# A fused two-layer attention, mixture and feed-forward kernel: late expert weights in halves, rows two tiles ahead, projections two heads earlier

## The reference, cut to what matters

```python
x = x + L0_xattn(layernorm(x), ctx, ctx, mask, ...)   # 16 heads of 16, over the 256 positions of a sequence
x = x + L0_ffn(layernorm(x), router_w, ...)           # 16 experts, top 4 of each token, hidden 256
x = x + L1_xattn(layernorm(x), ctx, ctx, ...)         # 16 heads of 16, over the 16 sequences at one position
x = x + L1_ffn(layernorm(x), w_gate, w_up, w_down)    # silu gate, hidden 768
```

## Time and profile before

| | us |
|---|---|
| median of three runs | 1487.99 |
| the profiled execution | 1475.79 |
| its span, first to last instruction | 1473.9 |

### The profile page before, as it was taken

How to read it: one execution, slowest core, us unless ns; L and a number is a source line. 1 busy time by engine, 2 the same in 40 slices (tenths; PEclk the granted TensorE clock), 3 DMA queues, 4 the chain that set the end, 5 groups by cost and what they waited for, 6 DMA issues and landing times. The chain is left out here.

```text
span 1473.9 us, 34906 instructions
## 1 busy us (share of the span) xinstructions
PE 1153.6 (78%) x11011; PEld 871.1 (59%) x11012; DVE 972.4 (66%) x2207; ACT 741.7 (50%) x1455; POOL 825.2 (56%) x983
## 2 busy tenths in 40 slices
PE   3788999999860478899999996137887888849997
PEld 2456666666540366789998885125666666625554
DVE  4878878888630477566668894446777887426652
ACT  2367667676650255455555553114555666624442
POOL 5213366766576566577767772677667772005442
PEclk9889999999985699899999999577999999979999
DMA  6533442321110146543333342654475542122221
GB/s 181 123 94 99 123 91 73 91 80 51 43 41 8 49 143 155 84 124 114 114 114 110 100 115 72 144 137 123 131 202 141 140 131 64 42 72 72 86 71 58
DMA packets 138997, 147.59 MB, mean 100 GB/s; under 512 B 39848, under 2 KB 114648, under 8 KB 138840
## 3 DMA queue, kind: packets, MB, share of 16 engines
q1 hardware_dynamic: 112144, 95.45, 22.9%
q0 software_dynamic: 17920, 37.84, 11.1%
q10 hardware_dynamic: 8800, 12.59, 3.1%
HBM read 81.82 MB, written 38.40 MB: 82 GB/s over the span
## 5 line engine op out<-in xcount | busy, mean ns | idle before, releaser
L465 ACT ACTIVATE l_pt<-l_ps_t 128x512 f32<-128x512 f32 (+1 forms) x512 | 242.8, 492 | 222.0 <-PE l_ps_t L882 214.3
L735 DVE TENSOR_REDUCE l_mx<-l_ps_s 128x2 f32<-128x512 f32 (+1 forms) x512 | 275.6, 549 | 106.5 <-PE l_ps_s L917 103.2
L1371 PE MATMUL cp_ps_g<-cp_xt,ro_wexp 128*128 128x256 f16 x1920 | 228.9, 277 | 27.0 <-ACT cp_xt L1311 17.1
L1371 PEld LDWEIGHTS cp_ps_g<-cp_xt,ro_wexp 128*128 x1920 | 185.6, 99 | 56.2 <-issue 32.8
L1229 POOL DMA_INDIRECT cp_rows<-moe_rows,cp_now x160 | 163.9, 1025 | 93.9 <-POOL cp_now L1224 66.1
L384 POOL DMA_INDIRECT l_picked<-expert_rows,l_slots x128 | 142.0, 1110 | 38.6 <-issue 37.2
L408 POOL DMA_INDIRECT row_tokens<-l_token_id,ro_pos x128 | 125.8, 983 | 42.4 <-issue 42.3
L1287 DVE TENSOR_SCALAR cp_gate<-cp_ps_g,ex_g_bias 128x256 f32<-128x256 f32 x160 | 69.9, 478 | 89.7 <-PE cp_ps_g L1371 89.7
L917 PE MATMUL l_ps_s<-ro_wexp 96*128 96x256 f16 x512 | 103.3, 287 | 25.1 <-issue 8.1
L1320 ACT CAST cp_a_hi<-cp_act_f 128x512 f16<-128x512 f32 x80 | 49.4, 618 | 142.1 <-DVE cp_act_f L1296 140.5
L1234 POOL TENSOR_TENSOR cp_a_lo<-cp_act_f,cp_a_hi 128x512 f16<-128x512 f32 x80 | 95.8, 1197 | 35.8 <-ACT cp_a_hi L1320 34.6
(11 more groups left out here) (246 smaller groups left out, 2835.5 us busy)
## 6 DMA issues: line engine op xcount, KB each, us to landing
expert_rows<-cp_yout SPq DMA_DIRECT2D x80, 256.0 KB
l_cin<-in_ctxT SPq DMA_DIRECT2D x32, 256.0 KB
x<-l_yout SPq DMA_DIRECT2D x64, 128.0 KB
ro_wexp<-l_nat SPq DMA_DIRECT2D x48, 128.0 KB
ro_wexp<-l_nat SPq DMA_DIRECT2D x96, 64.0 KB
l_qs<-l_nat SPq DMA_DIRECT2D x48, 128.0 KB
l_ks<-l_nat SPq DMA_DIRECT2D x96, 64.0 KB
ro_raw<-in_gate_up ACTq DMA_DIRECT2D x10, 512.0 KB, 4.7
```

The costliest lines, as they stand in the source:

```text
L465: nc.scalar.activation(pt[:, h % 8], ps_t[:, at % 2, :, 0:span], ACT.Exp).then_inc(exp_done, 1)
L735: nc.vector.reduce_max(mx[:, n % 2, :, 8 * (k % 2) + k // 2], ps_s[:, at % 2, :, 0:span], AX_X).then_inc(max_done, 1)
L1371: last = nc.tensor.matmul(ps_g[:, b, m], route.wexp[:, bass.ds(e, 1), cols:cols + P].rearrange("p o n -> p (o n)"), xt[:, b, part, c], sta ...
```

## The change

1. Layer 0: experts 0 to 7 are split one at the end of each of the iterations u = 1 to 8, and experts 8 and 9 are loaded in u = 10 (before: u = 3).
2. Both attentions: the transposes of x move from k = 0 to k = 15 of the iteration before; high and low of x from k = 1 to k = 0, q products to k = 2, 3, their high and low to k = 4. The k products start at K_AT (7 in layer 0, 6 in layer 1; before 8), their high and low at K_AT + 2, v products at K_AT + 4, the copy to `v1` at K_AT + 6.
3. Layer 0, GpSimd: the eight scatters stand together at the end of the iteration, and for unit u-3 (before: four and four, for u-4).
4. Layer 1: VectorE makes `invert` and `weigh` of k = 5 ahead of that head's `add_expert`. GpSimd sets its constants in u = -4 (before: -5), and there the gather comes ahead of `first_norm`.
5. Expert tiles: late experts are split in halves, one half (gate and up, or down) a step, from step -2 to step 13; the low half stands behind tile i's work on VectorE. ScalarE's order in step i is sigmoid of i, high half, copy of tile i+2's rows, a_hi of i, output of i-2. The down weights get their own load semaphore.

```diff
-        EXPERTS_AT = {-3: (0,), -2: (1, 2), -1: (3, 4), 0: (5, 6), 1: (7,)} if routing else {}
+        EXPERTS_AT = {u: (u - 1,) for u in range(1, EARLY + 1)} if routing else {}
...
+        K_AT = 7 if routing else 6
...
-                    if routing and live(u - 4):
-                        scatter(u - 4, 0)
-                    if u > -5:
-                        if u > -4:
-                            gather(u + 5)
+                    if routing:
                         first_norm(u + 4)
                         if u == -4:
-                            gather(u + 5)
-                            if routing:
-                                constants()
+                            constants()
                     else:
                         gather(u + 5)
-                        if not routing:
+                        if u == -4:
                             constants()
+                        first_norm(u + 4)
...
-                    if routing and live(u - 4):
-                        scatter(u - 4, 1)
+                    if routing and live(u - 3):
+                        for q in range(QT):
+                            scatter(u - 3, q)
...
-                        n = u + 3
-                        if k == 0 and live(n):
+                        n = u + 4
+                        if k == 15 and live(n):
                             pe.wait_ge(xn_done, c1 + 2 * n + 2)
                             pe.wait_ge(v1_done, c1 + n)
...
-                        if k in (8, 9) and live(n):
+                        if k in (K_AT, K_AT + 1) and live(n):
                             pe.wait_ge(clo_done, c1 + n + 1)
                             pe.wait_ge(ql_done, c1 + n + 1)
...
-                return EARLY + i // 2 if isinstance(i, int) and i % 2 == 0 and 0 <= i // 2 < LATE else None
+                return EARLY + (i + 2) // 2 if isinstance(i, int) and 0 <= (i + 2) // 2 < LATE else None
...
+                        e = late_expert(i)
+                        if e is not None:
+                            dve.wait_ge(e_high, i + 3)
+                            part = 1 + 2 * (i % 2)
+                            nc.vector.scalar_tensor_tensor(route.part(e, part), route.raw_parts(e)[i % 2], WS, route.part(e, part - 1), ALU.mult, ALU.subtract).then_inc(e_low, 1)
...
                     def step(i, b4):
                         b = b4 % 2
-                        if live(i, 1):
-                            act.wait_ge(xt_done, at(i + 1))
-
-                            act.wait_ge(gu_done, at(i - 1))
-                            nc.scalar.copy(xt[:, 1 - b], ps_x[:, 1 - b]).then_inc(xt_copied, 1)
+                        if isinstance(i, int) and i == -2:
+                            copy_rows(0, 0)
                         if live(i, 0):
                             act.wait_ge(gate_done, at(i, 2))
 
                             act.wait_ge(act_done, at(i - 2))
                             nc.scalar.activation(sg[:, b], gate[:, b], ACT.Sigmoid, scale=ALPHA / WS).then_inc(sg_done, 1)
+                        split_half(i)
+                        if live(i, 2) and (not isinstance(i, int) or i > -2):
+                            copy_rows(i + 2, b)
+                        if live(i, 0):
                             act.wait_ge(act_done, at(i))
```

More of the change, by code:

```diff
@@ L519, in step @@
                             norm_high(u - 2)
-                        if k == 1 and live(u + 3):
+                        if k == 0 and live(u + 3):
                             act.wait_ge(xt_done, c1 + u + 4)
@@ L547, in step @@
                         n = u + 3
-                        if k == 14 and live(n):
+                        if k == K_AT + 6 and live(n):
                             act.wait_ge(v_done, c1 + n + 1)
@@ L559, in step @@
                         if k == 8:
-                            for e in EXPERTS_AT.get(u, ()) + ((EARLY, EARLY + 1) if routing and u == 3 else ()):
+                            for e in EXPERTS_AT.get(u, ()) + ((EARLY, EARLY + 1) if routing and u == EARLY + 2 else ()):
                                 if e >= 2:
@@ L753, in step @@
                         n = u + 3
-                        if k == 1 and live(n):
+                        if k == 0 and live(n):
                             dve.wait_ge(xhi_done, c1 + n + 1)
@@ L764, in step @@
                                                            ALU.mult, ALU.subtract).then_inc(ml_done, 1)
+                        if k == 5 and live(u - 1):
+                            invert(u - 1, 1)
+                            weigh(u - 1, 1)
                         filling = adding and u < -2
@@ L770, in step @@
                                 add_expert(u + 4, k - 12)
-                        if k == 5 and live(u - 1):
-                            invert(u - 1, 1)
-                            weigh(u - 1, 1)
-                        if k == 6 and live(u + 3):
+                        if k == 4 and live(u + 3):
                             project_low(u + 3, 1, qh_done, ps_b, bq, qs_stacked, ql_done)
@@ L1276, in step @@
                         b = b4 % 2
-                        e = late_expert(i - 1)
-                        if e is not None:
-                            dve.wait_ge(e_high, 2 * (e - EARLY) + 2)
-                            for part, raw in zip((1, 3), route.raw_parts(e)):
-                                nc.vector.scalar_tensor_tensor(route.part(e, part), raw, WS, route.part(e, part - 1), ALU.mult, ALU.subtract).then_inc(e_low, 1)
                         if live(i, 0):
@@ L1304, in _, with copy_rows, split_half, load_half @@
                 def _(act):
+                    def copy_rows(i, b):
+                        act.wait_ge(xt_done, at(i))
+                        act.wait_ge(gu_done, at(i - 2))
+                        nc.scalar.copy(xt[:, b], ps_x[:, b]).then_inc(xt_copied, 1)
+                    def split_half(i):
+                        e = late_expert(i)
+                        if e is not None:
+                            if e < EARLY + 2:
+                                act.wait_ge(bank.named(f"e_loaded{e % 2}"), 32 * (e // 2 + 1))
+                            elif i % 2 == 0:
+                                act.wait_ge(e_loaded[e % 2], 32 * ((e - EARLY) // 2))
+                            else:
+                                act.wait_ge(d_loaded[e % 2], 16 * ((e - EARLY) // 2))
+                            nc.scalar.activation(route.part(e, 2 * (i % 2)), route.raw_parts(e)[i % 2], ACT.Copy, scale=WS).then_inc(e_high, 1)
+                    def load_half(i):
+                        e = late_expert(i)
+                        if e is not None and e + 2 < E:
+                            act.wait_ge(e_low, i + 3)
+                            if i % 2 == 0:
+                                for c in range(KC):
+                                    route.load_gate_up(act, e + 2, c, e_loaded[e % 2])
+                            else:
+                                route.load_down(act, e + 2, d_loaded[e % 2])
                     def step(i, b4):
                         b = b4 % 2
-                        if live(i, 1):
-                            act.wait_ge(xt_done, at(i + 1))
-                            act.wait_ge(gu_done, at(i - 1))
-                            nc.scalar.copy(xt[:, 1 - b], ps_x[:, 1 - b]).then_inc(xt_copied, 1)
+                        if isinstance(i, int) and i == -2:
+                            copy_rows(0, 0)
                         if live(i, 0):
@@ L1325, in step @@
                             nc.scalar.activation(yout[:, b], ps_y[:, b], ACT.Copy, scale=1.0 / WS).then_inc(y_copied, 1)
[L1326 to L1341 removed]
+                        load_half(i - 1)
                     run(act, [xt_copied, sg_done, ahi_done, y_copied], step)
```

34 lines of the change are left out of this document (10 added, 24 removed).

## The result

The changed kernel takes 1503.77 us in the median (1503.25 to 1509.85), the kernel before, run beside it, 1486.72 (1481.43 to 1493.13). The ratio is 1.014, 95% interval 1.0105 to 1.0183: slower, where 1427 was forecast. The profiled execution took 1509.85 us, 34 more than that of before (1475.79), twice what the medians differ by. Two of them (loads_only, tiles_start) are of executions over 1.5% above the fastest of their kernel, and their stages are read as upper values only.

What follows compares the result with a forecast made beforehand. No one engine bounds the program; each stage has its own limit. Terms -8 - 6 + 0 - 23 + 9 - 5 - 22 = -55 from the profiled 1475.8 give 1421, plus 6 for the median: 1427 us; eight in ten, 1402 to 1452.

Steps and rivals of the forecast that it cites:

- I take 1 us for each of the five more, half of what the low part lasts, since TensorE has two scores in hand: Layer 0's units: experts split at five more unit ends cost 5 us, set against a gain of 11.
- the gain (-11): Layer 0's units: 23.15 us a unit could fall at most 0.9, to GpSimd's loop of 22.2, over 12 units.
- layer 1's units (-22: Layer 1: waits for DMAs into `ks` and `an` mostly go, GpSimd late next at 17.2; 17.4 us a unit, 2.0 by 11.
- Rival (b): Both attentions held by GpSimd and ScalarE loops: layer 0 loses 3, layer 1's units go to 18.4; 1447 us, chance 0.18.
- the loop through the eight scatters: Layer 0's units: GpSimd and ScalarE loop of xn, eight scatters, second scale and shift, `norm_again` takes 22.2 us.
- rival (e): Layer 0: runs of eight scatters stop 5.26 us in each of 15 units; slower, about 1498 us, chance 0.03.
- The tiles' head (-23: Expert tiles 0 to 15: waits for copied rows and last low part go; 4.87 us a tile, 98 to 75 us.
- rival (c): Expert tiles' head: VectorE bounds it at 5.5 us a tile, 10 us more; 1437 us, chance 0.08.
- Behind the head (+9: Expert tiles after the head: slow pace of 4.87 us from the head on, 36 more tiles by 0.26, 9 us lost.
- Start of layer 1 (-5): Layer 1's start: gather ahead of first norm brings TensorE's transposes of unit 1 5 to 6 us earlier; 5 us gained.
- Layer 0's end (0): Layer 0's end: eight fewer scatters left (10 us) and a longer GpSimd loop in short last iterations about cancel.
- The first iterations (-8): Layer 0, u = -3 to 0: seven experts leave, products come earlier; 2.5 us each for u = -2 to 0, 0.5 for -3.

Runs made afterwards that it cites:

- loads_only: undo_experts plus one unused 768 KB load a unit issued by ScalarE in u = 2 to 8, experts 8 and 9 loaded in u = 10: ratio 0.9984.
- tiles_start: Kernel before with the expert tiles' change and layer 1's new first iterations (constants in u = -4, gather ahead of first norm): ratio 0.9885, 1476.6 us.
- undo_experts: Changed kernel with experts 0 to 7 split as before (u = -3 to 1), experts 8 and 9 loaded in u = 3: ratio 0.9881, 1481.0 us.
- only_tiles: Kernel before with only the expert tiles' change (halves, rows copied two tiles ahead): ratio 0.9916, 1483.5 us.
- alo_early: undo_experts with a_hi and low part of the attention output at k = 8, ahead of k's projections (before k = 9): ratio 0.9716, 1456.0 us.
- splits_only: Changed kernel without the loads of experts 2 to 7, data of experts 0 and 1 split in their stead: ratio 0.9983, 1485.1 us.

## Why the prediction was wrong

**The step that failed first is "I take 1 us for each of the five more, half of what the low part lasts, since TensorE has two scores in hand".** It had priced a split at the unit's end by VectorE's time alone. What stood in its place: for splits, 2.5 to 2.7 us of TensorE's standing for `an` in each of eight units, since `an` and not only a score is behind the low part, and the low clock after it. The loads that move with the splits had no price at all in the sum: in the trace of before each issue lasted half a us, but in iterations that have no scatters. Together these two made some 45 us of the 62, where 5 had been taken. Of the other 16 it stays open how much is the change's. Some 9 are u = 4 (31.6 us in undo_experts, 22.5 before), which is as long in every kernel with the early projections; but only_tiles, whose layer 0 is that of before, took 299.1 us too, so 283.1 was a short one.

The move also cost more in the new order (1.7 to 2.6%) than in the old (0.5%). I think it is in part because the early projections had taken cover from alo: in layer 0 one of the two k products, 1.2 us, stands now ahead of ScalarE's issue at k = 8, where both stood behind it. The waits at like issues agree, but no run separates it, and the issues were longer in the new order as well.

**In the same stretch, the gain (-11) was mis-sized before anything was set against it.** The 23.15 us of "today's unit" were read from 93.5 us on and have the first iterations' splits in them; the ten units from 124.7 to 350.2 take 22.55. Against the loop's 22.2 that leaves 0.35 a unit, 4 us in twelve, and the loop came out at 22.8, so none.

**Second, layer 1's units (-22, came out at +2.9).** Two waits were taken as gone with "late next is GpSimd" at 17.2 us a unit. The late next was alo, not on layer 1's list of before at all, because both k products stood in front of it: 19.8 us, with 15.2 for the low parts of q and k. GpSimd was not the bound: it waited 3.4 us a unit for ScalarE's xn. The price of the removed waits was nearer: with alo early, 15 of the 22 us came (273.3 to 258.5), with most units of 17.7 to 18.8 us against the 17.4 taken. None of the five rivals was this one. Rival (b) had layer 1 held at 18.4, but by GpSimd.

**Layer 0's late units without experts** were held as said, by the loop through the eight scatters, `shift2` and `norm_again`: 22.3 to 22.8 us, where 22.2 had been summed. The units u = 2 to 5 were not (24.3 to 28.9 in undo_experts). The slower rival (e), scatters that stop, did not come: they last 0.96 us with 0.30 between, as before, but for one stop of 3.0 us at the end. That its 1498 us lies near the measured 1504 is chance.

**The tiles' head (-23, measured -17.4)** was mis-sized: a tile takes 80.6/15 = 5.37 us, not 4.87. The wait for `cp_xt` went, as said (TensorE's longest wait in the stretch is now the first row below); then came rival (c), VectorE as the bound, at nearly its 5.5 us a tile. It is busy in nearly all of the stretch, 79.2 us where the same work had been 69.5 before (second row):

```profile
PE cp_ps_y L1394 <- POOL cp_a_lo L1233: 9.8, 11, 1.6
...
556.80:637.40 80.60, 69.40 (x662) 58.48 (x662) 79.15 (x108) 47.62 (x70) 63.59 (x59) 1.00 0.53 139
```

One of its instructions is longer than the 1.97 us that was taken (count, ns min/median/max). The rule cited in the prediction (the Trainium skill, page "SBUF — State Buffer", section "Who interferes with whom") gave an estimate of 1.85; the trace agrees with it in kind, but has 2.25, 0.4 us more:

```profile
L1285 DVE SCALAR_TENSOR_TENSOR cp_up<-cp_up,cp_gate x13: 691/2253/2268, 563.2 to 630.6; 128x512 f32<-128x512 f32 x13
```

**Behind the head (+9, measured +1.6).** The slow pace did not begin there, behind a stand of TensorE's at tile 18 for the gathers; that GpSimd caught up in it is my reading, and no run tries it:

```profile
651.49 1.03 PE L1367 MATMUL cp_ps_x<-ex_ident,cp_rows 128*128 128x128 f16 x8 [2.39 <-DMA cp_rows<-moe_rows,cp_now]
```

```profile
L1285 DVE SCALAR_TENSOR_TENSOR cp_up<-cp_up,cp_gate x36: 691/692/1340, 658.0 to 818.8; 128x512 f32<-128x512 f32 x36
```

In six of the experiments with the new tiles this stretch took 307 to 311 us, and in six 302 to 304 (before 300.1, with the slow pace in tiles 54 to 75), so which pace sets in isn't fixed by the change; +9 was one end and not the middle.

**Start of layer 1 (-5)** was right (-5.1), and the runs show its cause, the order of the gather. **Layer 0's end (0)** came out at -2.8.

**The first iterations (-8)** were mis-sized, and only luck makes -7.4 look like it. The forecast summed u = -3 to 0, most of which lies ahead of the table's second row; there the change gained 9 us, hidden by the later start, and then 7.4 in u = 0 and 1, 16 in all. The other traces agree: from the first issue of down weights to unit 2's first maximum it takes 59 to 62 us in the seven kernels with experts as before and 49 to 52 in the eight with one a unit.

## What to carry to other kernels

A wait's price is only gained if the next one isn't right behind it: before products are moved away, look at what is made beside them (here a_hi and alo during the k products), and move that too. Work moved into a full stage is priced by who stands behind it in its own engine's stream, at the very place where it is put; the same splits cost some 25 us at the units' ends and next to nothing six heads later. And a DMA issue is an instruction of the engine that makes it: keep it off an engine on which the chain depends, all the more where other queues are at work.

## What the runs showed of the hardware

A DMA issue of ScalarE can hold it for long. The issues of `in_down` lasted 0.5 to 0.7 us ahead of a kernel's first scatter, but for one of 1.6 in alo_early. Behind it, in the five kernels with such a load from ScalarE in most units, 23 of 35 lasted 1.3 to 8.4 us (loads_only: 0.6 or less up to 189 us, then 2.3, 1.7, 3.1, 2.3, 2.9 and 0.5). SyncE's, between its own DMAs, lasted 0.5 to 1.3. During the 8.44 us the DMA engines were busy in most slices and moved almost nothing (the row is tenths of busy time in 40 slices of 182 to 191, and the mean of that stretch):

```profile
DMA  9999999900956900940999099000099099009040
...
DMA packets 92, 0.12 MB, mean 13 GB/s; under 512 B 18, under 2 KB 68, under 8 KB 90
```

The packets themselves show the same order in time, in all fifteen traces, also without a load there (splits_only): from 60 us on, none that starts ahead of the first scatter takes over 1.8 us, and behind it the longest take 3.3 to 10.7 us. Why they take so long, and whether it is the scatters that cause it, was not tried; only the order in time is shown.

TensorE's clock fell to 1.2 GHz at each of the eight stands of 2.5 to 2.7 us for `an` and at three for alo (3.2, 3.7 and 8.8 us), in units where it had been at 2.4 GHz throughout before: of the 7.1 us that a unit of layer 0 lost, 2.8 are the same work at the lower clock and not waiting.

One VectorE instruction, the mask's bias above, lasted 0.69 us in the six traces where it ended ahead of GpSimd's two memsets, and 6.4 to 8.1 in the nine where it ran beside them. That moves all that follows by 9 us, and the instruction's start ranged only from 13.1 to 17.2 us.
